# Projections of four attention stages: f32 products against three f16 products of split operands

## The chip, the core and the metric

One Trainium2 chip, one of its cores, one launch. The metric is the device time of that launch in microseconds (us).

## The reference, cut to what matters

Two decoder layers on `x` (8 blocks of 112 tokens, 256 wide) and a context (8 blocks of 375 tokens, 192 wide). Layer 0: feature-map attention, cross attention with a small feed-forward part, eight experts of which two serve each token. Layer 1 begins with squared-score attention, then wide cross attention, then causal attention with four small experts:

```python
# squared-score attention, 16 heads, 16 wide keys, 64 wide values
q, k, v = x @ Wq.T, x @ Wk.T, x @ Wv.T                 # 256, 256, 1024 wide
A = tril(1 + q.k / 4 + (q.k / 4) ** 2 / 2)
y = rms_norm(A @ v, per head) * g_weight
x = layernorm(x + y @ Wo.T)                            # 1024 -> 256
# wide heads: 16 heads, 64 wide, over the 375 context tokens
q = x @ w_q                                            # 256 -> 1024
x = layernorm(x + softmax(q.k / 8) @ v @ w_out + b)    # 1024 -> 256
# causal heads: 16 heads, 16 wide, rms norm in front and on queries and keys
h = rms(x) * n1_w
q, k, v = h @ wq.T, h @ wk.T, h @ wv.T                 # 256 each
```

The matrices named above, and the same `x` in front of them, are what the change is about.

## The kernel before, in words

A planner (`step`, `place`, `weave`, `rest`, `until`) writes one ordered list of units for each stage, `plans[0]` to `plans[5]`. Each engine (TensorE, ScalarE, VectorE, GpSimd, and SP, which issues most DMAs) walks the same list and issues its own part of every unit, so each engine's queue is strictly in the order of the list, and a wait holds everything behind it on that engine. Streams are woven by planned costs in ns (the last argument of `step`); `rest(ns)` lets so much planned cost pass before a stream goes on, and `REST` is 1500. Between two stages stands a fence: `end_stage` notes the last result of each of the four computing engines, and every engine waits for all of them (`fence`) before its first unit of the next stage.

**Stage 2** (`plans[2]`, to about 421 us of the profile) runs the eight experts. Its expert products are already three f16 products of split operands: a value times `WSCALE` is cast to f16, the rest of the cast is a second f16 tensor, and `PARTS` names the pairs high x high, high x low, low x high. Its last units are the last expert's output, and `get` 0 to 3, GpSimd's gathers of the experts' rows. The weights of the next stage are loaded by SP in `w3in`, and the context key weights are split in `wk4` (L1819, L1934).

**Stage 3** (`plans[3]`, 421 to 662 us) is the squared-score attention. First come the value units of the wide heads (`v4`, 5 products of 512 columns each, evicted by ScalarE at L624 and stored by DMA through four buffers), 18 of them ahead of the first `qk3`. Between them `combine` adds the gathered rows on VectorE (L2255), `norm` normalizes, and `xT`, `xTe` turn a block of `x` through TensorE into `x_ch`, channels on partitions, f32 (L587, ScalarE at L630). Then for each pair of blocks `qk3` (queries and keys, 224 columns), for each block `v3` (values, 512 columns), `s3` and `y3` (scores and sums), `turn3`, `sq3`, `rms3`, `scale3` (norm of the heads), `yT3`, `yT3e` (the turn of y into `s3_yT`, f32, ScalarE at L2242), and `out` (8 f32 products of 256 columns), followed by `norm` and the turn of the new `x`. The units `k4` (context keys of the wide heads, 5 f16 products of 375 columns) fill in between, and `wo3` lets GpSimd scale the output weight by `g_weight` once (L2313). All of `qk3`, `v3`, `out` and `q4` are f32 products; `mm` (L398) records all of them. Bank ring `misc3` has four banks.

**Stage 4** (`plans[4]`, 662 to 1024 us) weaves the wide heads with the causal ones. For each pair of heads: `sc4` (scores, L2604), the maximum on VectorE (L2684), the exponential on ScalarE (L2653), `nm4` (normalization on VectorE, L2695), `trA4`, `trV4` (turns, L2612, evicted by ScalarE at L2645 and by VectorE at L2676), `av4` (L2623); for each four pairs `oT4` (ScalarE evicts half a block's output into `s4_attT`, L2661); for each block `out`, `norm`, `xT`. `q4` makes the queries of two blocks. After a block's `norm` the causal heads follow: `qkv5` (three f32 projections of 256 columns), `ms5` (the mean squares on VectorE, and their power on GpSimd, L2985), `qk5`, `qkT5`, `s5`, `pT5`, `av5` and the rest. `n15` lets GpSimd scale the three weights of `qkv5` (L2714). `ffnin` loads the last stage's weights in three groups after the last `av4`.

**The order around the wide output.** `s4_out` waits in the plan for the second `oT4` of its block, then `rest(REST / 2)`, then places `out`. In the steady part of the list the units run `ms5` of an earlier block, `av4`, `oT4`, `sc4`, `pT5`, `av4`, `out`.

```python
def s4_out(b):
    yield from until(("oT4", b, 1))
    yield from rest(REST / 2)
    yield [("out", 4, b)]
    yield from norm_and_turn(4, b, pace=0.5)
```

## Time and profile before

| | |
|---|---|
| runs | 1168.29, 1170.60, 1169.72 us; median 1169.72 |
| profiled execution | span 1165.0 us (first to last instruction); its whole time is not listed apart from the three runs |
| instructions | 21556, of them 8624 matmul records |
| stage 3 | 421 to 662 us |
| stage 4 | 662 to 1024 us |

The times of the profile are microseconds from the first instruction. TensorE stands in two lines, PE for matmuls and PEld for weight loads, which overlap. DVE is VectorE, ACT is ScalarE, POOL is GpSimd. An f32 matmul of the program leaves two records, an f16 one leaves one. In brackets behind a row stands the idle time of the engine ahead of it and what ended it. The line number is the one of the helper that issues the instruction, so the tiles have to be read too: `w_Wo,s_yT` is the output of the squared-score heads, `w_Wv,x_ch` their values, `w_Wo,s_attT` the output of the wide heads, `x_ch,w_Wq` a query projection.

### The profile page before, as it was taken

How to read it: one execution, taken by the hardware profiler on the slowest of the kernel's cores; microseconds unless marked ns; L12 is line 12 of the kernel's file. 1: busy time of each engine (PE TensorE's matmuls, PEld its weight loads, DVE VectorE, ACT ScalarE, POOL GpSimd, SP SyncE). 2: the span in 40 equal slices, each digit the busy share in tenths (PEclk: the TensorE clock that was granted, in tenths of full speed). 3: DMA queues.
4: the chain of work that ended last, by engine and by line, in shares of the span. 5: the costliest groups of instructions: out<-in, count | busy, mean ns of one | idle time of the engine just before them, and what ended most of it. 6: DMA issues, size and time to landing. Idle time of an engine off the chain costs nothing.

```text
span 1165.0 us, 21556 instructions
## 1 busy us (share of the span) xinstructions
PE 1001.8 (86%) x8624; PEld 707.4 (61%) x8624; DVE 640.4 (55%) x1519; ACT 588.3 (50%) x1374; POOL 284.6 (24%) x292
## 2 busy tenths in 40 slices
PE   7996898887689988789998799889888897789995
PEld 4664565665388854456655676667666665447654
DVE  3246545666669833454455476776676664527003
ACT  5532565552468844344544354556555544465741
POOL 2521412100500033211112202221132124132733
PEclk9988889898989999899999988999999888679998
DMA  9341464102679785422252243313222105000001
GB/s 311 99 86 40 112 127 110 45 12 98 209 272 314 259 278 168 139 88 85 80 173 88 81 120 105 101 34 107 81 57 78 27 1 226 1 1 1 1 1 32
DMA packets 66676, 123.68 MB, mean 106 GB/s; under 512 B 11632, under 2 KB 41968, under 8 KB 62496
## 3 DMA queue, kind: packets, MB, share of 16 engines
q1 hardware_dynamic: 64528, 117.48, 33.0%
q0 software_dynamic: 2048, 4.82, 1.4%
q8 instruction: 68, 1.11, 0.4%
q14 instruction: 32, 0.26, 0.1%
HBM read 86.30 MB, written 35.92 MB: 105 GB/s over the span
## 4 chain that ended last, share of the span: by engine, by line
PE 56%; DVE 19%; ACT 11%; DMA 5%; issue 4%; POOL 4%; SPq 1%; another core or an unknown queue 0%; DVEq 0%; ACTq 0%; POOLq 0%
PE psum L398 38%; DVE s_p L2695 3%; ACT s_p L2653 3%; POOL rs L2985 2%; PE psum L2612 2%; DVE s_max L2684 2%; PE psum L2623 2%; PE psum L1369 2%; PE psum L2784 1%; DVE s_pT L2676 1%; PE psum L550 1%; DVE s_max L653 1%; PE psum L2173 1%; PE psum L2159 1%; PE psum L2604 1%
## 5 line engine op out<-in xcount | busy, mean ns | idle before, releaser
L2653 ACT ACTIVATE s_p<-psum,s_max 112x375 f32<-112x375 f32 x128 | 72.3, 569 | 87.6 <-DVE s_max L2684 87.6
L693 POOL TENSOR_TENSOR rstd<-meanvar,minus_half 112x1 f32<-112x1 f32 x40 | 23.1, 578 | 279.6 <-DVE meanvar L645 209.9
L653 DVE TENSOR_REDUCE s_max<-psum 112x2 f32<-112x750 f32 x64 | 59.4, 935 | 32.5 <-PE psum L550 31.4
L2985 POOL TENSOR_TENSOR rs<-ms,minus_half 112x32 f32<-112x32 f32 x8 | 43.5, 5442 | 110.3 <-DVE ms L2919 110.3
L398 PE MATMUL psum<-Wv,ctx 128*125 128x512 f16 x240 | 59.6, 392 | 11.2 <-ACT s_v L624 5.4
L398 PE MATMUL psum<-ctx,Wk 128*128 128x375 f16 x320 | 62.8, 331 | 5.0 <-ACT s_yT L2242 2.8
L2684 DVE TENSOR_REDUCE s_max<-psum 112x1 f32<-112x375 f32 x128 | 63.7, 539 | 2.3 <-PE psum L2604 2.1
L2612 PE MATMUL psum<-ident,s_p 112*125 112x112 f32 x384 | 61.4, 294 | 3.9 <-DVE s_p L2695 2.3
L609 ACT ACTIVATE s_k<-psum 128x375 f16<-128x375 f32 x64 | 31.2, 488 | 62.1 <-PE psum L398 59.5
L2604 PE MATMUL psum<-s_k,s_q 64*112 64x375 f16 x384 | 46.0, 345 | 17.0 <-ACT s_p L2653 6.5
L2612 PEld LDWEIGHTS psum<-ident,s_p 112*125 112x125 f32 x384 | 51.7, 198 | 13.7 <-DVE s_p L2695 3.9
L3303 POOL TENSOR_TENSOR hidden<-raw,hidden 128x448 f16<-128x448 f32 x44 | 45.6, 1036 | 54.4 <-ACT hidden L3186 52.7
L1431 ACT ACTIVATE s_pT<-psum 125x672 f32<-125x672 f32 x64 | 46.6, 730 | 22.8 <-PE psum L1357 21.2
L2623 PE MATMUL psum<-s_pT,s_v 125*64 125x112 f32 x768 | 53.9, 278 | 4.4 <-ACT s_attT L2661 4.4
L677 DVE SCALAR_TENSOR_TENSOR s_k<-psum,s_k 128x375 f16<-128x375 f32 x64 | 34.8, 546 | 36.2 <-ACT s_k L609 35.8
L624 ACT ACTIVATE s_v<-psum 125x512 f32<-125x512 f32 x48 | 28.3, 596 | 49.2 <-PE psum L398 33.4
L2623 PEld LDWEIGHTS psum<-s_pT,s_v 125*64 125x64 f32 x768 | 39.7, 143 | 20.1 <-issue 17.3
L398 PEld LDWEIGHTS psum<-Wv,ctx 128*125 128x125 f16 x240 | 32.1, 141 | 32.3 <-issue 9.6
L2695 DVE TENSOR_SCALAR s_p<-s_p,s_sum 112x375 f32<-112x375 f32 x128 | 49.3, 427 | 2.3
L3275 DVE SCALAR_TENSOR_TENSOR x_tok<-psum,wt,x_tok 112x192 f32<-112x192 f32 x32 | 12.6, 414 | 68.7 <-PE psum L398 68.6
L2645 ACT ACTIVATE s_pT<-psum 125x336 f32<-125x336 f32 x64 | 29.0, 453 | 38.3 <-PE psum L2612 38.2
L398 PE MATMUL psum<-x_ch,w_Wq 128*128 128x224 f32 x192 | 46.3, 382 | 2.1 <-ACT x_ch L630 1.5
(360 smaller groups left out, 2445.1 us busy)
## 6 DMA issues: line engine op xcount, KB each, us to landing
keys<-s_k SPq DMA_DIRECT2D x64, 187.5 KB, 2.2
s_k<-keys SPq DMA_DIRECT2D x8, 1500.0 KB, 7.6
values<-s_v SPq DMA_DIRECT2D x48, 224.0 KB
s_v<-values SPq DMA_DIRECT2D x16, 672.0 KB
raw_wg<-in_wg SPq DMA_DIRECT2D x8, 1024.0 KB, 6.6
raw_wu<-in_wu SPq DMA_DIRECT2D x8, 1024.0 KB, 7.1
raw_wd<-in_wd SPq DMA_DIRECT2D x8, 1024.0 KB
s_kd<-k_halves SPq DMA_DIRECT2D x48, 93.8 KB, 3.8
```

The costliest lines, as they stand in the source:

```text
L398: ins = TE.matmul(bank, left, right, start=i == 0, stop=last)
L653: VE.tensor_reduce(s1_max[b % 2][:, 2 * p:2 * p + 2], rings["s1"][unit][0:N, :, 0:S], X, ALU.max, negate=True).then_inc(*V.up("max1", n))
L677: VE.scalar_tensor_tensor(t[:, 1, :], rings["misc3"][unit][:, 0:S], 1 / WSCALE, t[:, 0, :], ALU.mult, ALU.subtract).then_inc(*V.up("k4", *at))
L1431: SC.activation(rings["pT1"][n], rings["s1"][unit][0:SCH, :, 0:NCH * N], ACT.Exp, scale=0.25).then_inc(*A.up("exp1", n))
L2604: ins = TE.matmul(rings["s4"][(n, j)][0:N, 0:S], q[rows, p, u, cols(b % 2)], k[rows, p, v, :], start=i == 0, stop=i == 2)
L2612: ins = TE.transpose(rings["t4"][unit][0:SCH, c * N:(c + 1) * N], p[:, c * SCH:(c + 1) * SCH], ident[0:N, 0:N])
L2623: ins = TE.matmul(rings["o4"][n // 4][64 * j:64 * j + 64, p % 4 * N:(p % 4 + 1) * N], s4_v[n // 4 % 3][:, c, 2 * (p % 4) + j, :], rings["p ...
L2653: SC.activation(rings["p4"][2 * n + j], rings["s4"][(n, j)][0:N, 0:S], ACT.Exp, bias=s4_max[b % 2][:, h:h + 1], accum_out=s4_sum[b % 2][:, ...
L2684: VE.tensor_reduce(s4_max[b % 2][:, h:h + 1], rings["s4"][(n, j)][0:N, 0:S], X, ALU.max, negate=True).then_inc(*V.up(name, n))
L2695: VE.tensor_scalar(t, t, sums[:, j:j + 1], None, ALU.mult).then_inc(*V.up(name, n))
L2985: GP.tensor_tensor(rs5[b % 2][:], ms5[b % 2][:], minus_half[:], ALU.pow).then_inc(*G.up("rs5", b))
L3303: GP.tensor_tensor(dst[:, 1, f, :], raw_, dst[:, 0, f, :], ALU.subtract).then_inc(*G.up("ll", *at))
```

## The change

All projections named in the reference above become three f16 products each. `x_ch` gives way, from the turn after the experts on, to `x16` in the same bytes: ScalarE casts the turned block to f16, VectorE writes the rest (`xH`, `xHe`); `s3_yT` is split in the same way (`yT3e` on both engines). The four weights of stage 3 are split by ScalarE and VectorE at the end of stage 2 (`w3s`, with `g_weight` in the scale of `Wo3`, so that `wo3` goes), those of the wide heads in stage 3 (`w4s`, after `out` of blocks 2 and 3), the three of the causal heads by GpSimd in `n15`, one block earlier than before. The output of the wide heads stays f32 in `s4_attT` and is split by GpSimd, a cast and a subtraction for each half (`oT4`); `out` waits for GpSimd and is placed `1.5 * REST` after `oT4`. Scales by 1/WSCALE go into the evictions. The third group of the last weights waits for the last wide `out`.

```diff
+    halves = Region(nc, keep.base + keep.at, KC * T_ * 4)
     x_ch = keep.tensor("x_ch", [P, KC, T_])
+    x16 = halves.tensor("x16", [P, 2, KC, T_], F16)
...
+    W3_16 = Region(nc, ringm.base + 28 * KB, 20 * KB)
+    w3_16 = {name: W3_16.tensor(name + "_16", shape, F16) for name, shape in (
+        ("Wv3", [P, 2, KC, HW]), ("Wq3", [P, 2, KC, D]), ("Wk3", [P, 2, KC, D]),
+        ("Wo3", [P, 2, HW // P, D]))}
...
-        return A["xT", s, b] if s >= 0 else g_x.ready
+        return V["xH", s, b] if s >= 2 else A["xT", s, b] if s >= 0 else g_x.ready
...
+    step("xH", "T xH", "misc#", "V xH", cost=250)
+    step("xHe", "A xH, V xH")
...
-            pe.wait_ge(x_ch_at(3, b), x_ch_at(3, b + 1), g_w4.ready, *ring.free(unit))
-            mm(ring[unit][:, 0:2 * N], [(Wq4[:, k, t * P:(t + 1) * P], x_ch[:, k, b * N:(b + 2) * N])
-                                        for k in range(KC)], T.up("q4", s, b, t))
+            pe.wait_ge(x_ch_at(3, b), x_ch_at(3, b + 1), V["w4s", "Wq4"], *ring.free(unit))
+            mm(ring[unit][:, 0:2 * N],
+               [(w4_16["Wq4"][:, u, k, t * P:(t + 1) * P], x16[:, v, k, b * N:(b + 2) * N])
+                for k in range(KC) for u, v in PARTS], T.up("q4", s, b, t))
...
+        if what == "xHe":
+            s, b = at
+            bank = rings[f"misc{s}"][("xH", s, b)]
+            act.wait_ge(T["xH", s, b])
+            SC.activation(x16[:, 0, :, cols(b)],
+                          bank[:, 0:KC * N].rearrange("p (t n) -> p t n", n=N),
+                          ACT.Copy).then_inc(*A.up("xH", s, b))
...
+    def vector_add_scaled(s, b, base, base_at, y):
+
+        dve.wait_ge(T["out", s, b], base_at)
+        VE.scalar_tensor_tensor(res[:, b, :], y, 1 / WSCALE, base[:, b, :], ALU.mult,
+                                ALU.add).then_inc(*V.up("nadd", s, b))
         dve.wait_ge(V["nadd", s, b])
         vector_moments(s, b, res)
...
+        if what == "xHe":
+            s, b = at
+            dve.wait_ge(A["xH", s, b])
+            VE.scalar_tensor_tensor(
+                x16[:, 1, :, cols(b)],
+                rings[f"misc{s}"][("xH", s, b)][:, 0:KC * N].rearrange("p (t n) -> p t n", n=N), 1.0,
+                x16[:, 0, :, cols(b)], ALU.mult, ALU.subtract).then_inc(*V.up("xH", s, b))
...
+    place(("g3",))
+    for name in ("Wq3", "Wk3", "Wv3", "Wo3"):
+        place(("w3s", name))
...
+            elif what == "w3s":
+                name, = at
+                act.wait_ge(g_w3.ready, T["down", E0 - 1], V["g3",])
+                SC.activation(w3_16[name][:, 0], w3[name][:], ACT.Copy,
+                              scale=ch("g3") if name == "Wo3" else WSCALE).then_inc(*A.up("w3s", name))
...
+            elif what == "w3s":
+                name, = at
+                dve.wait_ge(A["w3s", name], V["g3",])
+                VE.scalar_tensor_tensor(w3_16[name][:, 1], w3[name][:],
+                                        ch("g3") if name == "Wo3" else WSCALE, w3_16[name][:, 0],
+                                        ALU.mult, ALU.subtract).then_inc(*V.up("w3s", name))
...
+    raw_w4 = Region(nc, wts.base + keys_at, 20 * KB)
+    w4_raw = {"Wq4": g_w4.load(raw_w4, "Wq4", [P, KC, HW]),
+              "Wo4": g_w4.load(raw_w4, "Wo4", [P, HW // P, D])}
+    w4_16 = {"Wq4": ringm.tensor("Wq4_16", [P, 2, KC, HW], F16),
+             "Wo4": ringm.tensor("Wo4_16", [P, 2, HW // P, D], F16)}
...
-        place(("wo3",))
...
+        yield from until(("out", 3, 2))
+        yield [("w4s", "Wq4")]
+        yield from until(("out", 3, 3))
+        yield [("w4s", "Wo4")]
...
-                pe.wait_ge(g_w3.ready, x_ch_at(2, b), x_ch_at(2, b + 1), *rings["misc3"].free(unit))
-                for w, at_ in ((Wq3, 0), (Wk3, 2 * N)):
+                pe.wait_ge(x_ch_at(2, b), x_ch_at(2, b + 1), *rings["misc3"].free(unit))
+                for name, at_ in (("Wq3", 0), ("Wk3", 2 * N)):
                     mm(bank[:, at_:at_ + 2 * N],
-                       [(w[:, k, c * P:(c + 1) * P], x_ch[:, k, b * N:(b + 2) * N])
-                        for k in range(KC)], T.up("qk3", b, c) if at_ else None)
+                       [(w3_16[name][:, u, k, c * P:(c + 1) * P], x16[:, v, k, b * N:(b + 2) * N])
...
-                   [(x_ch[:, k, cols(b)], Wv3[:, k, c * 512:(c + 1) * 512]) for k in range(KC)],
-                   T.up("v3", b, c))
+                   [(x16[:, u, k, cols(b)], w3_16["Wv3"][:, v, k, c * 512:(c + 1) * 512])
+                    for k in range(KC) for u, v in PARTS], T.up("v3", b, c))
...
-                pe.wait_ge(A["yT3", b, 4], G["wo3",], *rings["misc3"].free(unit))
+                pe.wait_ge(V["yT3", b, 4], *rings["misc3"].free(unit))
                 mm(rings["misc3"][unit][0:N, 0:D],
-                   [(s3_yT[b % 2][:, k, :], Wo3[:, k, :]) for k in range(HW // P)], T.up("out", 3, b))
+                   [(s3_yT[b % 2][:, u, k, :], w3_16["Wo3"][:, v, k, :])
+                    for k in range(HW // P) for u, v in PARTS], T.up("out", 3, b))
             else:
...
+            elif what == "yT3e":
+                b, t0 = at
+                bank = rings["misc3"][("yT3", b, t0)]
+                dve.wait_ge(A["yT3", b, t0])
+                VE.scalar_tensor_tensor(s3_yT[b % 2][:, 1, t0:t0 + 4, :],
+                                        bank[:, 0:4 * N].rearrange("p (t n) -> p t n", n=N), 1.0,
+                                        s3_yT[b % 2][:, 0, t0:t0 + 4, :], ALU.mult,
+                                        ALU.subtract).then_inc(*V.up("yT3", b, t0))
...
+            elif what == "w4s":
+                name, = at
+                act.wait_ge(g_w4.ready, V["got", 2, B - 1])
+                SC.activation(w4_16[name][:, 0], w4_raw[name][:], ACT.Copy,
+                              scale=WSCALE).then_inc(*A.up("w4s", name))
...
+            elif what == "w4s":
+                name, = at
+                dve.wait_ge(A["w4s", name])
+                VE.scalar_tensor_tensor(w4_16[name][:, 1], w4_raw[name][:], WSCALE, w4_16[name][:, 0],
+                                        ALU.mult, ALU.subtract).then_inc(*V.up("w4s", name))
...
-            elif what == "wo3":
-                pool.wait_ge(g_w3.ready)
-                GP.tensor_scalar(Wo3[:], Wo3[:], ch("g3"), None, ALU.mult).then_inc(*G.up("wo3"))
...
+                sp.wait_ge(V["got", 2, B - 1])
...
-    step("oT4", "A oT4")
+    step("oT4", "A oT4, G +1, G oT4")
     step("w5in")
-    step("n15", "G +5, G n15")
+    step("n15", "G +9, G +2, G n15")
 
...
+        if b == 1:
+            place(("w5in",))
         if b == 2:
-            place(("w5in",))
+            place(("n15",))
         if b == 3:
-            place(("n15",))
             place(("ones5",))
...
-        yield from rest(REST / 2)
+        yield from rest(1.5 * REST)
...
-                pe.wait_ge(A["oT4", b, 1], *rings["misc4"].free(unit))
+                pe.wait_ge(G["oT4", b, 1], V["w4s", "Wo4"], *rings["misc4"].free(unit))
                 mm(rings["misc4"][unit][0:N, 0:D],
-                   [(s4_attT[:, k, :], Wo4[:, k, :]) for k in range(HW // P)], T.up("out", 4, b))
+                   [(s4_att16[:, u, k, :], w4_16["Wo4"][:, v, k, :])
+                    for k in range(HW // P) for u, v in PARTS], T.up("out", 4, b))
             elif what in UNITS5:
...
-                    act.wait_ge(T["out", 4, b - 1])
+                    act.wait_ge(G["oT4", b - 1, q])
...
+            elif what == "oT4":
+                b, q = at
+                half = slice(4 * q, 4 * q + 4)
+                if b:
+                    pool.wait_ge(T["out", 4, b - 1])
+                pool.wait_ge(A["oT4", b, q])
+                GP.tensor_copy(s4_att16[:, 0, half, :], s4_attT[:, half, :]).then_inc(*G.up())
+                pool.wait_ge(G.so_far())
+                GP.tensor_tensor(s4_att16[:, 1, half, :], s4_attT[:, half, :], s4_att16[:, 0, half, :],
+                                 ALU.subtract).then_inc(*G.up("oT4", b, q))
...
-                        w = ffn_w[name][:, c, :]
-                        GP.tensor_scalar(w, w, ch("n1", c), None, ALU.mult).then_inc(
-                            *(G.up("n15") if (name, c) == ("wv5", KC - 1) else G.up()))
+                        w = w5[name][:, c, :]
+                        GP.tensor_scalar(w, w, ch("n1", c), WSCALE, ALU.mult,
+                                         ALU.mult).then_inc(*G.up())
+                for name in ("wq5", "wk5", "wv5"):
+                    pool.wait_ge(G.so_far())
+                    GP.tensor_copy(w5_16[name][:, 0], w5[name][:]).then_inc(*G.up())
+                    pool.wait_ge(G.so_far())
+                    GP.tensor_tensor(w5_16[name][:, 1], w5[name][:], w5_16[name][:, 0],
+                                     ALU.subtract).then_inc(*(G.up("n15") if name == "wv5" else G.up()))
...
-                for group in ffn_groups:
+                for group in ffn_groups[:2]:
                     group.start()
+                sp.wait_ge(T["out", 4, B - 1])
+                ffn_groups[2].start()
...
-                   [(x_ch[:, k, cols(b)], ffn_w[w][:, k, :]) for k in range(KC)],
-                   T.up("qk5", b) if j else None)
+                   [(x16[:, u, k, cols(b)], w5_16[w][:, v, k, :])
+                    for k in range(KC) for u, v in PARTS], T.up("qk5", b) if j else None)
             pe.wait_ge(*ring.free(("vv5", b)))
             mm(ring[("vv5", b)][0:N, 0:D],
-               [(x_ch[:, k, cols(b)], ffn_w["wv5"][:, k, :]) for k in range(KC)], T.up("v5", b))
+               [(x16[:, u, k, cols(b)], w5_16["wv5"][:, v, k, :])
+                for k in range(KC) for u, v in PARTS], T.up("v5", b))
```

## Rows read from the trace of the kernel before

**Rows 1.** The page, part 1: busy time, its share of the span, instructions.

```profile
PE 1001.8 (86%) x8624; PEld 707.4 (61%) x8624; DVE 640.4 (55%) x1519; ACT 588.3 (50%) x1374; POOL 284.6 (24%) x292
```

**Rows 2.** The page, part 4: the chain that ended last, by engine.

```profile
PE 56%; DVE 19%; ACT 11%; DMA 5%; issue 4%; POOL 4%; SPq 1%; another core or an unknown queue 0%; DVEq 0%; ACTq 0%; POOLq 0%
```

**Rows 3.** Windows: stretch, length, busy us (instructions) by engine, PEclk, DMA share, GB/s.

```profile
490.00:640.00 150.00, 139.05 (x915) 87.79 (x916) 75.58 (x153) 68.87 (x149) 23.61 (x13) 1.00 0.32 103
640.00:662.00 22.00, 16.15 (x88) 13.49 (x88) 8.65 (x23) 6.73 (x18) 4.26 (x4) 1.00 0.03 10
...
760.00:960.00 200.00, 177.09 (x1560) 131.66 (x1556) 138.15 (x369) 111.34 (x362) 45.40 (x35) 0.96 0.19 55
960.00:1024.00 64.00, 45.65 (x296) 32.23 (x294) 28.05 (x60) 28.32 (x88) 19.88 (x17) 0.72 0.26 103
```

**Rows 4.** Timeline, TensorE, squared-score stage: start, us, line, what, records.

```profile
562.11 3.71 PE L398 MATMUL psum<-w_Wo,s_yT 128*112 128x256 f32 x16
...
572.39 1.02 PE L398 MATMUL psum<-x_ch,w_Wq 128*128 128x224 f32 x4
...
574.01 0.96 PE L398 MATMUL psum<-ctx,Wk 128*128 128x375 f16 x5
...
576.72 1.88 PE L398 MATMUL psum<-w_Wv,x_ch 128*112 128x512 f32 x4
```

**Rows 5.** Timeline, TensorE, queries of the wide heads, at the stage end.

```profile
645.25 3.95 PE L398 MATMUL psum<-x_ch,w_Wq 128*128 128x224 f32 x20
```

**Rows 6.** Timeline, TensorE, wide-head stage.

```profile
803.23 1.03 PE L398 MATMUL psum<-w_wk,x_ch 128*112 128x256 f32 x4
...
813.68 3.71 PE L398 MATMUL psum<-w_Wo,s_attT 128*112 128x256 f32 x16
```

**Rows 7.** Timeline, TensorE, f16 products of 256 columns.

```profile
137.37 0.71 PE L398 MATMUL psum<-Wkv,ctx 128*125 128x256 f16 x5
```

**Rows 8.** Timeline, TensorE, around the stage boundary.

```profile
421.32 8.82 PE L398 MATMUL psum<-Wv,ctx 128*125 128x512 f16 x40 [0.79 <-PE psum L1761]
...
449.92 0.99 PE L398 MATMUL psum<-x_ch,w_Wq 128*128 128x224 f32 x4 [1.46 <-ACT x_ch L630]
...
454.10 1.24 PE L398 MATMUL psum<-Wv,ctx 128*125 128x512 f16 x5
```

**Rows 9.** Timeline, ScalarE, around the stage boundary.

```profile
414.80 1.99 ACT L1819 ACTIVATE Wk<-Wk 128x1024 f16<-128x1024 f32 x2
...
420.63 0.59 ACT L1812 ACTIVATE e_out<-psum 70x512 f32<-70x512 f32 x1 [0.78 <-PE psum L1761]
```

**Rows 10.** Timeline, VectorE, around the stage boundary.

```profile
416.82 1.23 DVE L1934 SCALAR_TENSOR_TENSOR Wk<-Wk,Wk 128x1024 f16<-128x1024 f32 x1 [2.19 <-ACT Wk L1819]
...
430.94 0.48 DVE L2255 SCALAR_TENSOR_TENSOR res<-got,w_k,x_tok 112x256 f32<-112x256 f32 x1 [11.11 <-issue]
...
471.54 3.23 DVE L2277 SCALAR_TENSOR_TENSOR s_a<-s_a,half_causal 112x448 f32<-112x448 f32 x2 [1.68 <-ACT s_a L2221]
```

**Rows 11.** Timeline, GpSimd, around the stage boundary.

```profile
424.04 1.02 POOL L1965 DMA_INDIRECT got<-expert_out,get_i  x1 [52.23 <-DMA expert_out<-e_out]
...
470.03 5.45 POOL L2313 TENSOR_SCALAR w_Wo<-w_Wo,chan 128x2048 f32<-128x2048 f32 x1
```

**Rows 12.** One line (L2277): ns min/median/max of its instructions.

```profile
L2277 DVE SCALAR_TENSOR_TENSOR s_a<-s_a,half_causal x32: 611/622/2693, 462.7 to 626.2; 112x448 f32<-112x448 f32 x32
```

**Rows 13.** One line (L683): ns min/median/max.

```profile
L683 DVE SCALAR_TENSOR_TENSOR s_q<-psum,s_q x32: 379/391/393, 647.0 to 800.6; 128x224 f16<-128x224 f32 x32
```

**Rows 14.** Groups of GpSimd, by form: line, op, xcount, busy us, mean ns, idle.

```profile
L3303 POOL TENSOR_TENSOR hidden<-raw,hidden 128x448 f16<-128x448 f32 x44 | 45.6, 1036 | 54.4 <-ACT hidden L3186 52.7
...
L710 POOL CAST ctx<-ctx_raw 128x375 f16<-128x375 f32 x8 | 4.0, 499 | 27.9 <-DMA ctx_raw<-in_ctxT 19.8 <-PE psum L1357 8.1
```

**Rows 15.** Timeline, GpSimd, wide-head stage.

```profile
811.20 5.44 POOL L2985 TENSOR_TENSOR rs<-ms,minus_half 112x32 f32<-112x32 f32 x1 [17.54 <-DVE ms L2919]
```

**Rows 16.** Timeline, ScalarE, wide-head stage.

```profile
812.22 0.58 ACT L2661 ACTIVATE s_attT<-psum 128x448 f32<-128x448 f32 x1
```

69 lines of the change are left out of this document (42 added, 27 removed).

## The prediction, made before the changed kernel was run

> **What bounds the kernel now.** I read the busy shares first: TensorE 86%, every other engine far below [rows 1]. Then the chain that ended last: TensorE 56%, VectorE 19%, ScalarE 11% [rows 2]. TensorE is the first suspect, but almost half of the chain is somebody else's latency. So I cut the two stages that the change touches into windows [rows 3]. The squared-score stage is dense from 490 to 640 us (139.05 of 150 us busy, full clock) and loose at its end, 640 to 662 (16.15 of 22), where the last block goes through its chain alone. The wide-head stage has 177.09 of 200 us of TensorE, but VectorE has 138.15 beside it, and its 23 us of idle lie scattered between heads. Its tail, 960 to 1024, has TensorE busy 45.65 of 64 us at a mean clock of 0.72: latency again.
>
> A difference of 0.2% (2.3 us) is about what a measurement of this kernel can tell from none. The profiled span is 1165.0 us; its whole time is not listed. The three runs have a median of 1169.72, 4.7 above that span, and I sum against 1169.7.
>
> **What the products save.** A run in the timeline overlaps its successor by 0.16 us (its last end is modelled), so a run costs its length less 0.16. Each f32 matmul leaves two records.
> - Old output projection, 8 matmuls of 256 columns: 3.71 - 0.16 = 3.55 us; old values, 2 of 512 columns: 1.88 - 0.16 = 1.72; old query and key pair: 574.01 - 572.39 = 1.62 [rows 4]. Old wide queries: (3.95 - 0.16) / 5 = 0.76 each [rows 5]. One of the three last projections: 1.03 - 0.16 = 0.87; the wide output is again 3.55 [rows 6].
> - New price: an f16 product of 256 columns steps at (0.71 - 0.16) / 5 = 0.110 us [rows 7], one of 512 at (1.24 - 0.16) / 5 = 0.216 [rows 8]. Between them lies 0.41 ns a column, so 224 columns are 0.110 - 0.013 = 0.097.
>
> Three products replace each matmul:
> - squared-score output: 24 x 0.110 = 2.64 for 3.55, saves 0.91, x8 = 7.3
> - its values: 6 x 0.216 = 1.30 for 1.72, 0.42 x16 = 6.7
> - its queries and keys: 12 x 0.097 = 1.16 for 1.62, 0.46 x8 = 3.7
> - wide queries: 0.58 for 0.76, 0.18 x32 = 5.8, of which 8 units (1.4) fall in the squared-score stage and 24 (4.3) behind it
> - wide output: 0.91 x8 = 7.3
> - queries, keys, values of the causal heads: 18 x 0.110 = 1.98 for 2.61, 0.63 x8 = 5.0
>
> That is 19.1 us in the squared-score stage and 16.6 in the wide-head stage, 35.7 in all. Three quarters is what the rows give. The Trainium skill (FP8 and Floating Point Precision, TensorE Precision Notes) has f32 as four passes; three f16 passes are then exactly 25% less, and the rows agree within a few per cent.
>
> How much reaches the end? In the dense stretch TensorE idles 7%, so I take 0.9: 17 us (bounds 12 and 19). In the wide-head stage 11% idle sits between exponentials and maxima that the products don't shorten, so I take 0.75: 12.5 us (bounds 0, if the head loop is latency, and 19, with the halved clock of some stretches).
>
> **What it adds at the stage boundary.** The four weights of the squared-score stage are now split ahead of a fence that all engines wait for. ScalarE can begin after its last expert eviction, 421.2. It casts 5120 columns; two of 1024 took 1.99 us [rows 9], so 5.0 us, until 426.2. VectorE follows at 1.23 us per 1024 [rows 10]; its last 2048 begin after the last cast and end near 428.7. TensorE, which now starts 8 value units (40 products) at 421.32 [rows 8], idles 7.5 us. Is that the price? The layer's first combine waits for gathered rows until 430.94 [rows 10] on gathers that GpSimd issues from 424.04 [rows 11]; they are ahead of the fence and stay. But the first query unit, at 449.92, has 18 value units in front of it on TensorE. 428.7 + 18 x 1.08 = 448.1, plus 0.8 for turns and 1 for the split of x: 450, if the stores of the values keep up; in the kernel before the stretch of 18 units took 28.6 us instead of 20, and the clock may start low. Bounds 0 and +8; I take +4, the middle, since part of the old 28.6 us was the combine and part the stores.
>
> **Smaller terms.** GpSimd's scaling of the output weight goes, 5.45 us at 470.03 [rows 11]. During it a VectorE pair at 471.54 took 3.23 us [rows 10]; its instructions are 622 ns at the median and 2693 at most [rows 12]. That is 2 us on a stretch that TensorE waited for: -2 (bounds -3 and 0). The wide heads' two weights are split inside the stage: 2 casts of 1.9 us on ScalarE, 2 splits of 2.4 on VectorE, in queues ahead of key evictions; four banks cover about 3 us: +2 (0 to +5). Every turned block of x gets a VectorE split of 0.39 us [rows 13], 24 in all, every turned half of y one near 0.62 [rows 12], 16 in all; inside the dense stretch VectorE is half idle and they are covered, but in the last blocks' chains they are on the path: +2 (+1 to +5). The cast of x stays the same on ScalarE. SP's load of the wide weights now waits for the last combine, which is over by then: 0. The third group of the last weights waits for the last wide output; its queue is still busy with the first two: 0. The last projections' weights are split by GpSimd earlier, with one block more of lead: 0.
>
> **The wide heads' output, the new wait.** ScalarE evicts, then GpSimd casts (499 ns for 375 columns, so 0.6 for 448) and subtracts (1.036) [rows 14], and only then may TensorE run the output. The queue of GpSimd matters: its power of 5.44 us starts at 811.20 [rows 15], ScalarE evicts the block's second half at 812.22 [rows 16]; in five more blocks (from 737, 769, 851, 889 and 930 us) the same two stand within 1.2 us. So the split begins at 816.7 and ends at 818.4. The output stood at 813.68 [rows 6]. The order now places it behind 1500 planned ns more, about one transposed group, one attention step and one score, 2.6 us of TensorE: 816.3. TensorE then stands still 2.1 us, 6 times, 12.6 us, and scores, attention and turns of later heads are queued behind it. Some of that fills gaps that would come anyway: I take +9 (0 to +33). The 32 new GpSimd instructions also stand beside VectorE's: +2 (0 to +26). The tail after the last head: split of the attention +1.7, split of x +0.4, shorter products -1.5, later start of the last block's output: +1.
>
> **Sum.** 1169.7 - 17 - 12.5 + 4 - 2 + 2 + 2 + 9 + 2 + 1 = 1158.2; I say 1158.
>
> **The rivals.**
> - *The whole gain arrives.* The order moves the output far enough to hide the split, and gaps close: 1169.7 - 35.7 - 2 + 4 = 1136. For it: GpSimd is busy 24% and TensorE 86% [rows 1]. Against: gaps of latency. 20%.
> - *The head loop is latency.* The wide-head stage gives nothing back: 1158 + 12.5 = 1170.5. For it: TensorE has only 56% of the chain [rows 2]. 13%.
> - *Slower: the power in front of the split.* If the output keeps its real place, TensorE waits from 813.7 to 818.4, 4.7 us in 7 blocks, 33 us in place of 9: 1182. It decides from about 3.5 us of wait a block. For it: six blocks show the pair; against: three times the rest is planned ahead of the output. 12%.
> - *VectorE held up while GpSimd works.* One instruction was held 2 us beside a long one of GpSimd [rows 12]. Each block half would hold VectorE 1.64 us, 26 in all; half of it on the path is 13 in place of 2: 1169. Against: the normalization of the scores reads one tensor. The Trainium skill (SBUF — State Buffer, SBUF: two separate sides) speaks against this change: the port pair that VectorE and GpSimd share is an exclusive lock held for a whole instruction, taken by VectorE in a two-port mode or with two SBUF inputs. By that rule the 3.23 us are a lock (the trace agrees: 2693 ns for 622), and the new work would block alike. 11%.
> - *The forecast.* 44%.
>
> That the products aren't what they say can be left out: the lists are written out.
>
> **How the numbers follow.** Faster takes the forecast, the whole gain and a third each of the two rivals near 1170: 72%. Same 9%. Slower: the power, and the rest of those two, 19%. The range reaches from just above the whole gain to just above the latency case: 1140 to 1173.
>
> **What would show it.** Runs of 24 f16 records of 2.8 us for each output; the squared-score stage, from its first query unit to its end, shorter by 15 to 19 us; a first query unit between 450 and 458; TensorE idle ahead of the wide output, released by GpSimd, near 2 us in six blocks; VectorE's longest instructions beside GpSimd's copies no longer than 1 us. The forecast is wrong if that wait is absent or near 5 us, if the two stages shrink by much less than their products, or if the first query unit comes after 460.

## The result, and the profile after

The changed kernel takes 1201.61 us (median of 4 runs, 1198.83 to 1203.88) beside 1169.46 (4 runs), a ratio of 1.0252, 95% interval 1.0212 to 1.0292: **2.5% slower**, where 1158 was forecast and nothing above 1173 was in the range.

The page, part 1, of the changed kernel:

```profile
PE 992.4 (83%) x8928; PEld 711.2 (59%) x8928; DVE 671.4 (56%) x1566; ACT 592.9 (49%) x1380; POOL 309.4 (26%) x329
```

Beside [rows 1], TensorE is busy 9.4 us less and the span is 36.6 us longer. To find the place I cut both executions at the same events: the last eviction of expert outputs; the first query unit of the squared-score stage (its eviction, by VectorE); the first score of a wide head; the last transpose ahead of the last stage. Windows of the kernel before, squared-score and wide stretch (columns as in [rows 3]; the first number behind the bracket of GpSimd is PEclk, the clock that TensorE was granted, as a share of full speed):

```profile
451.70:661.70 210.00, 186.66 (x1151) 118.90 (x1150) 103.62 (x216) 88.47 (x193) 35.62 (x21) 0.98 0.30 97
661.70:1022.20 360.50, 309.97 (x2544) 229.70 (x2544) 234.21 (x613) 189.12 (x601) 83.13 (x73) 0.90 0.26 82
```

The changed kernel, boundary, squared-score and wide stretch:

```profile
425.10:463.30 38.20, 24.70 (x111) 14.70 (x112) 15.06 (x30) 16.56 (x25) 19.48 (x20) 0.87 0.65 199
463.30:688.30 225.00, 183.11 (x1292) 123.25 (x1290) 118.09 (x248) 91.54 (x195) 32.12 (x20) 0.91 0.27 90
688.30:1058.80 370.50, 301.52 (x2703) 228.16 (x2704) 244.13 (x621) 186.49 (x601) 110.01 (x111) 0.87 0.26 80
```

The boundary took 31.1 us before, the rest after the wide stretch 142.8 in both. So +7.1 at the boundary, +15.0 in the squared-score stretch, +10.0 in the wide one: 32.1, and the medians differ by 32.15. (The code ahead of the first cut is the same and took 420.6 and 425.1 us; over all executions below 415.6 to 426.2, so I take that part for scatter and compare stretches.)

Each stretch splits into TensorE's work at full clock (busy x granted clock, which its two digits give to about 1 us in the first stretch and 1.7 in the second), what the lower clock adds, and idle:

| | work | busy | clock | idle |
|---|---|---|---|---|
| squared-score, before | 182.9 | 186.7 | 0.98 | 23.3 |
| squared-score, after | 166.6 | 183.1 | 0.91 | 41.9 |
| wide, before | 279.0 | 310.0 | 0.90 | 50.5 |
| wide, after | 262.3 | 301.5 | 0.87 | 69.0 |

The products saved what they should: 16.3 us of work in the first stretch and 16.7 in the second, where 19.1 and 16.6 were forecast. But idle rose by 18.6 and 18.5, and the lower granted clock took most of what the products had saved: 166.6/0.91 is 13 us more than 166.6/0.98, and 262.3/0.87 is 10 us more than 262.3/0.90. TensorE's waits, longest first, in the squared-score stretch of the kernel before (line, releaser, us, times, longest):

```profile
PE psum L398 <- ACT s_yT L2242: 6.4, 8, 1.5
PE psum L587 <- DVE x_tok L688: 2.5, 1, 2.5
...
PE psum L2189 <- ACT s_yT L2242: 2.2, 2, 1.6
PE psum L398 <- ACT x_ch L630: 2.1, 3, 1.0
...
PE psum L2159 <- ACT s_yT L2242: 2.0, 2, 1.0
```

and in that of the changed kernel:

```profile
PE psum L405 <- DVE s_yT L2371: 13.1, 8, 2.6
PE psum L405 <- DVE x L714: 5.9, 3, 3.5
PE psum L2216 <- DVE s_yT L2371: 5.2, 4, 1.9
PE psum L598 <- DVE x_tok L721: 4.3, 2, 2.5
PE psum L2246 <- DVE s_yT L2371: 3.8, 2, 2.2
```

L2371 is VectorE's subtraction of the turned y. Scores (L2216) and turns (L2246) don't read y at all: they wait for its **PSUM bank**, the slot of the ring `misc3` in which TensorE had left the turned y. So do most of the waits at L405, the line of all products: in the timeline six of its eight stand ahead of context keys and values (10.0 us), and only two ahead of an output (3.1 us, 1.6 before). In all, the waits that end with y's eviction grew from 10.6 us in 12 to 22.1 in 14. The bank was waited for before the change too. One such place in both kernels, TensorE (start, us, what, [idle before <- releaser]), before:

```profile
539.69 1.01 PE L2159 MATMUL psum<-s_q,s_k 32*112 32x224 f32 x8 [1.01 <-ACT s_yT L2242]
```

after:

```profile
550.81 1.01 PE L2216 MATMUL psum<-s_q,s_k 32*112 32x224 f32 x8 [0.71 <-DVE s_yT L2371]
...
556.29 1.61 PE L2216 MATMUL psum<-s_q,s_k 32*112 32x224 f32 x8 [1.89 <-DVE s_yT L2371]
```

and VectorE:

```profile
554.26 0.69 DVE L2347 TENSOR_REDUCE s_ms<-s_y 112x8 f32<-112x512 f32 x1
554.95 0.55 DVE L703 SCALAR_TENSOR_TENSOR s_k<-psum,s_k 128x375 f16<-128x375 f32 x1
555.53 0.17 DVE L2352 TENSOR_SCALAR s_ms<-s_ms 112x16 f32<-112x16 f32 x1
555.62 0.62 DVE L2371 SCALAR_TENSOR_TENSOR s_yT<-psum,s_yT 128x448 f16<-128x448 f32 x1
```

ScalarE's eviction from that bank ran 554.81 to 555.35. In the kernel before it freed the bank; now the bank stays until 556.24, and TensorE stands 1.89 us, of which about 1.0 would have been there with ScalarE's mark. The 0.89 us that are new are 0.62 of the subtraction itself and 0.27 in VectorE's queue. In the first 14 of the 16 halves the subtraction began 0.02 to 0.45 us behind ScalarE's end, 3.0 us in all, and took 8.6 us itself: it is mostly the length of the new reader that holds the bank, and not the queue in front of it.

The second new wait is for `x`: products wait 5.9 us for VectorE's half of it (L714), where they waited 2.1 for the eviction, and turns of `x` wait 4.3 us for VectorE's norm (L721), 2.5 before.

The boundary, TensorE:

```profile
424.40 0.63 PE L1799 MATMUL psum<-ident,e_dT 128*70 128x128 f32 x4 [1.04 <-ACT e_dT L1842]
433.29 8.54 PE L405 MATMUL psum<-Wv,ctx 128*125 128x512 f16 x30 [8.26 <-DVE Wo L1980]
...
461.99 0.73 PE L405 MATMUL psum<-x,Wq 128*128 128x224 f16 x6 [1.60 <-DVE x L714]
```

8.26 us idle (7.5 forecast), and the first 30 records come at 8.54 us, where 40 took 8.82 in [rows 8]. Windows right behind the idle time show why (changed kernel):

```profile
433.30:438.00 4.70, 4.70 (x14) 2.64 (x15) 2.77 (x8) 0.99 (x2) 3.48 (x5) 0.60 0.32 99
438.00:442.00 4.00, 3.82 (x18) 2.14 (x16) 2.73 (x9) 1.99 (x4) 3.41 (x4) 1.00 0.87 231
```

The granted clock is 0.60 in the first, most of it at the 1.2 GHz level, and 1.00 in the second.

The wide stage. TensorE:

```profile
854.35 2.83 PE L405 MATMUL psum<-Wo,s_att 128*112 128x256 f16 x24
...
1007.36 4.36 PE L405 MATMUL psum<-Wo,s_att 128*112 128x256 f16 x24 [2.72 <-POOL s_att L2799]
```

GpSimd:

```profile
845.65 5.44 POOL L3088 TENSOR_TENSOR rs<-ms,minus_half 112x32 f32<-112x32 f32 x1 [17.83 <-DVE ms L3022]
...
851.55 0.56 POOL L2797 CAST s_att<-s_attT 128x448 f16<-128x448 f32 x1
852.19 1.04 POOL L2799 TENSOR_TENSOR s_att<-s_attT,s_att 128x448 f16<-128x448 f32 x1
```

The pair behind the power is there as forecast, yet in most blocks TensorE does not wait: the later place hides it (7.1 us in 3 waits, L405 <- L2799, in the whole stretch). So what cost the rest of the 18.5 us of idle, and the clock? The waits name a part of it: causal scores wait 6.5 us for exponentials (L2885 <- L2735; 1.7 before), the causal turns 5.2 us for ScalarE (L2894 <- L2974; 0.6 before), while a wait of 5.1 us of the wide scores for VectorE is gone. The rest is spread over many short ones. VectorE at the same time:

```profile
851.63 1.81 DVE L2777 TENSOR_SCALAR s_p<-s_p,s_sum 112x375 f32<-112x375 f32 x2
```

An undisturbed pair takes 0.74 us, this one took 1.81 beside GpSimd's two instructions; over the kernel their mean rose from 427 to 481 ns, 6.9 us for 128 (441 in e2 and 484 in e6 below, which differ by GpSimd's split). The Trainium skill (SBUF — State Buffer, SBUF: two separate sides) describes a port pair shared by VectorE and GpSimd as an exclusive lock that is held for a whole instruction. The stretched pair agrees with a lock; "for a whole instruction" does not hold for every instruction here: beside GpSimd's power of 5.44 us, in the kernel before, eight such pairs took their 0.74 us each.

### The profile page after: what moved, and what is told of

The parts are those of the page before. It is cut to its first block, busy times and chain, and to the rows that moved or that the text cites. A ratio compares the mean times of both kernels' runs of the same rounds, so it can differ in the third digit from the quotient of the medians.

```text
span 1201.6 us, 22274 instructions
## 1 busy us (share of the span) xinstructions
PE 992.4 (83%) x8928; PEld 711.2 (59%) x8928; DVE 671.4 (56%) x1566; ACT 592.9 (49%) x1380; POOL 309.4 (26%) x329
## 4 chain that ended last, share of the span: by engine, by line
PE 53%; DVE 19%; ACT 12%; DMA 6%; issue 4%; POOL 4%; SPq 1%; another core or an unknown queue 0%; DVEq 0%; ACTq 0%; POOLq 0%
PE psum L405 36%; ACT s_p L2735 3%; DVE s_p L2777 3%; PE psum L2704 2%; PE psum L2693 2%; DMA raw_wd<-in_wd 2%; POOL rs L3088 2%; DVE s_max L2766 2%; PE psum L2885 1%; PE psum L1402 1%; PE psum L2216 1%; DVE s_pT L2758 1%; PE psum L2230 1%; DMA values<-s_v 1%; PE psum L2685 1%
## 5 line engine op out<-in xcount | busy, mean ns | idle before, releaser
L2735 ACT ACTIVATE s_p<-psum,s_max 112x375 f32<-112x375 f32 x128 | 72.1, 568 | 100.1 <-DVE s_max L2766 100.1
L726 POOL TENSOR_TENSOR rstd<-meanvar,minus_half 112x1 f32<-112x1 f32 x40 | 24.8, 620 | 270.9 <-DVE meanvar L671 197.5
L405 PE MATMUL psum<-Wv,ctx 128*125 128x512 f16 x240 | 62.7, 409 | 17.2 <-DVE Wo L1980 8.3
L405 PE MATMUL psum<-ctx,Wk 128*128 128x375 f16 x320 | 66.5, 346 | 10.1 <-DVE s_yT L2371 6.6
L620 ACT ACTIVATE s_k<-psum 128x375 f16<-128x375 f32 x64 | 31.1, 487 | 66.9 <-PE psum L405 66.5
L2693 PEld LDWEIGHTS psum<-ident,s_p 112*125 112x125 f32 x384 | 53.5, 206 | 17.2 <-DVE s_p L2777 8.7
L2704 PE MATMUL psum<-s_pT,s_v 125*64 125x112 f32 x768 | 56.5, 287 | 5.9 <-ACT s_attT L2743 5.9
L2777 DVE TENSOR_SCALAR s_p<-s_p,s_sum 112x375 f32<-112x375 f32 x128 | 56.2, 481 | 2.3
L405 PEld LDWEIGHTS psum<-Wv,ctx 128*125 128x125 f16 x240 | 33.7, 147 | 39.0 <-issue 20.7
L703 DVE SCALAR_TENSOR_TENSOR s_k<-psum,s_k 128x375 f16<-128x375 f32 x64 | 34.7, 546 | 38.7 <-ACT s_k L620 38.2
L3378 DVE SCALAR_TENSOR_TENSOR x_tok<-psum,wt,x_tok 112x192 f32<-112x192 f32 x32 | 12.6, 414 | 68.7 <-PE psum L405 68.6
L405 PEld LDWEIGHTS psum<-ctx,Wk 128*128 128x128 f16 x320 | 30.1, 102 | 33.9 <-DVE s_yT L2371 8.1
L2727 ACT ACTIVATE s_pT<-psum 125x336 f32<-125x336 f32 x64 | 29.1, 455 | 37.2 <-PE psum L2693 37.1
```

The lines of the kernel that those rows point to most:

```text
L405: ins = TE.matmul(bank, left, right, start=i == 0, stop=last)
L703: VE.scalar_tensor_tensor(t[:, 1, :], rings["misc3"][unit][:, 0:S], 1 / WSCALE, t[:, 0, :], ALU.mult, ALU.subtract).then_inc(*V.up("k4", *at))
L2693: ins = TE.transpose(rings["t4"][unit][0:SCH, c * N:(c + 1) * N], p[:, c * SCH:(c + 1) * SCH], ident[0:N, 0:N])
L2704: ins = TE.matmul(rings["o4"][n // 4][64 * j:64 * j + 64, p % 4 * N:(p % 4 + 1) * N], s4_v[n // 4 % 3][:, c, 2 * (p % 4) + j, :], rings["p ...
L2735: SC.activation(rings["p4"][2 * n + j], rings["s4"][(n, j)][0:N, 0:S], ACT.Exp, bias=s4_max[b % 2][:, h:h + 1], accum_out=s4_sum[b % 2][:, ...
L2777: VE.tensor_scalar(t, t, sums[:, j:j + 1], None, ALU.mult).then_inc(*V.up(name, n))
```

## The experiments

Seventeen kernels ran, each with two timed executions or more (e2 and e11 with 8, e5 with 10, e16 with 11, e12 with 12). The stretches, each of one profiled execution, and the ratio of the times to the kernel before on the same chip:

| run | boundary | squared | wide | ratio (95%) |
|---|---|---|---|---|
| before | 31.1 | 210.0 | 360.5 | |
| after | 38.2 | 225.0 | 370.5 | 1.0252 (1.021-1.029) |
| e1_y_f32 | 34.4 | 210.2 | 369.6 | 1.0146 (1.004-1.025) |
| e2_wide_f32 | 36.7 | 224.8 | 345.2 | 1.0123 (1.007-1.018) |
| e3_four | 36.8 | 236.6 | 383.7 | 1.0514 (1.035-1.068) |
| e4_wo3_late | 34.5 | 228.6 | 370.5 | 1.0298 (1.019-1.041) |
| e5_both_f32 | 35.6 | 212.2 | 346.5 | 0.9982 (0.994-1.002) |
| e6_split_unused | 36.1 | 221.9 | 353.2 | 1.0148 (1.007-1.023) |
| e7_rest | 36.5 | 224.7 | 364.9 | 1.0249 (1.018-1.032) |
| e8_wide_sv | 37.3 | 222.7 | 362.1 | 1.0266 (1.020-1.033) |
| e9_split_early | 36.8 | 222.7 | 377.5 | 1.0377 (1.030-1.045) |
| e10_y_hold | 34.2 | 225.9 | 349.7 | 1.0101 (1.003-1.017) |
| e11_y_sbuf | 37.1 | 217.3 | 342.9 | 1.0061 (1.002-1.010) |
| e12_wide_queries | 31.0 | 216.6 | 347.8 | 0.9949 (0.992-0.998) |
| e13_late_even | 36.6 | 222.7 | 357.9 | 1.0224 (1.017-1.028) |
| e14_mid_even | 37.3 | 226.3 | 362.8 | 1.0246 (1.018-1.032) |
| e15_wide_f32_late_even | 37.4 | 220.9 | 360.4 | 1.0212 (1.015-1.027) |
| e16_queries_no_rest | 34.3 | 211.6 | 364.4 | 1.0081 (1.005-1.012) |
| e17_before_late | 37.2 | 210.9 | 370.8 | 1.0119 (1.004-1.020) |

How far is a stretch to be trusted? The same squared-score code (y split, Wo3 split ahead) took 220.9 to 226.3 us in nine executions, the same wide code 369.6 to 370.5 in three and 342.9 to 349.7 in four. The boundary of the kernel before took 31.1 and, in e17, 37.2; e12 and e16, with the same boundary, took 31.0 and 34.3. So a difference under 7 us between two stretches is not read by itself. The runs are of several chips, and a single profile can lie off its own times: that of e2 was 3.0 us longer than that of the kernel before, while its ratio says 14. So each main reading is given below by the ratios too; 1% is 11.7 us.

In the diffs, `...` stands for lines left out; they are against the changed kernel where nothing else is said.

**e1_y_f32**: y and the squared-score output product stay f32, the bank is released by ScalarE.

```diff
-    step("yT3", "T yT3", "misc3", "V yT3", 500)
-    step("yT3e", "A yT3, V yT3")
+    step("yT3", "T yT3", "misc3", "A yT3", 500)
+    step("yT3e", "A yT3")
...
-                   [(s3_yT[b % 2][:, u, k, :], w3_16["Wo3"][:, v, k, :])
-                    for k in range(HW // P) for u, v in PARTS], T.up("out", 3, b))
+                   [(s3_yT[b % 2][:, k, :], Wo3f[:, k, :])
+                    for k in range(HW // P)], T.up("out", 3, b))
```

> The squared-score output alone goes back to f32: y is turned and kept in f32, its bank is released by ScalarE, the output weight is one scaled f32 cast, and VectorE's 16 splits of y are gone; all else stays changed. Theory 1 (a turn's bank in the four-bank ring is now held until VectorE's split, TensorE stands still for it and its clock falls): the 22 us that TensorE waited for the split of y shrink to about 10 behind ScalarE's eviction, the mean granted clock from the first query unit to the stage's end rises from 0.91 to 0.96 or more, and the stage loses 10 to 18 us: about 1187. Theory 2 (fewer passes alone let the clock fall, waits are incidental): TensorE's work grows by 7 us, the waits don't matter, at most 4 us are gained: 1197 or more.

The stretch fell by 14.8 us, to 210.2, though its output products are longer again; by the ratios (1.0252 to 1.0146, with intervals that touch) it is 12. The granted clock is 0.96 for 0.91. The waits that end with y's eviction are back to 10.5 us, the longest group being (TensorE, squared-score stretch):

```profile
PE psum L406 <- ACT s_yT L2306: 6.3, 7, 1.5
```

That is the first theory. But 210.2 is also what the kernel before takes, with 11.8 us more of products in its stretch by the steps of the prediction: something besides y takes those.

**e2_wide_f32**: the wide output in f32 as before, without GpSimd's split, at its old place.

```diff
-    step("oT4", "A oT4, G +1, G oT4")
+    step("oT4", "A oT4")
...
-        yield from rest(1.5 * REST)
+        yield from rest(REST / 2)
...
-                   [(s4_att16[:, u, k, :], w4_16["Wo4"][:, v, k, :])
-                    for k in range(HW // P) for u, v in PARTS], T.up("out", 4, b))
+                   [(s4_attT[:, k, :], w4_16["Wo4"][:, k, :])
+                    for k in range(HW // P)], T.up("out", 4, b))
```

> The wide heads' output alone goes back to f32, without GpSimd's split and with the old rest ahead of it. Theory 1: the 7 us that TensorE waited for GpSimd's split go, and what the clock lost behind them; the wide-head stage (373 us, 363 before the change) comes back to 363 to 367: 1193 to 1197. Theory 2: the output is 0.9 us longer in each block and nothing else changes: 1205.

25.3 us less in the wide stretch, far more than either theory had; by the ratios, 1.0252 to 1.0123, it is 15. So this half of the change cost 15 to 25 us, although 7 us of saved product are in it.

**e3_four**: a fourth product (low by low) added to every split projection, work that the kernel does not need.

```diff
+FOUR = PARTS + ((1, 1),)
...
-                for k in range(KC) for u, v in PARTS]
+                for k in range(KC) for u, v in FOUR]
```

> Every changed projection gets the fourth product, low times low, so TensorE has the passes of f32 again (about 36 us more at full clock), with every wait of the change kept. Theory 1: the time is set by waits in part; the longer products are partly hidden and the clock is granted a little more often, so 10 to 25 us are added: 1212 to 1226. Theory 2: the clock comes back to 0.98 in the squared-score stage, which gives back what the products cost, so the time stays within 5 us of 1201.

By the steps of [rows 7, 8] it adds 35.6 us of TensorE, 18.6 and 17.0 in the two stretches; they grew by 11.6 and 13.2, 24.8 in all (30 by the ratios), as the first theory had it. TensorE's work does count, at 0.6 and 0.8 of its length. The gain was not lost because TensorE is off the path.

**e4_wo3_late**: the split of the squared-score output weight is moved behind the fence.

```diff
-    for name in ("Wq3", "Wk3", "Wv3", "Wo3"):
+    for name in ("Wq3", "Wk3", "Wv3"):
         place(("w3s", name))
...
         yield from until(("norm", 2, B - 1))
+        place(("wo3s",))
         place(("w4in",))
```

> The split of the squared-score output weight moves from ahead of the fence to where the kernel before scaled it (after the last norm of the layer before), so that the fence opens 1.9 us of ScalarE and 2.35 us of VectorE less late. Boundary theory: the first value unit and the first query unit come 2 to 4 us earlier, and the two instructions cost at most 1 us at their new place: 1197 to 1200. If the value units' stores or the combine set the first query unit, it stays at 36 us behind the start of the last expert eviction: 1201.

3.7 us less at the boundary and 3.6 more behind it, both under the scatter, and no difference in the time. The four kernels without VectorE's split of that weight ahead of the fence (e1, e4, e5, e10) have boundaries of 34.2 to 35.6, those with it 36.1 to 38.2: about 2 us.

**e5_both_f32**: e1 and e2 together.

> Both outputs (squared-score and wide) back to f32 with their old queues, all other projections stay f16 products. If the two costs are independent, the stages are those of the two single undoings: 210 us from the first query unit to the first score, 345 to the last stage; with 34 ahead and 143 behind them that is 12 us less than the same four stretches of the kernel before (744.4), so 1.0% faster than it, ratio 0.99. If the chip's clock or the ring simply shifts the idle time elsewhere, the sum stays above 740: ratio 1.0.

1162.87 us against 1163.95: no difference, over 10 and 13 runs, where the stretches of the two single undoings had promised 1%. So splitting the two outputs' operands, with the later place of the wide one, costs the whole 2.5%. But the other projections, 21.1 us of forecast product, bring nothing that the times can tell: their boundary is 4.5 us longer, their squared-score stretch 2.2 us longer, and only the wide one 14.0 shorter. Its windows, squared-score and wide:

```profile
461.10:673.30 212.20, 182.77 (x1229) 119.24 (x1228) 107.47 (x231) 91.28 (x195) 30.19 (x21) 0.94 0.29 95
673.30:1019.80 346.50, 290.90 (x2639) 217.39 (x2640) 237.65 (x621) 187.75 (x601) 84.95 (x79) 0.93 0.28 85
```

**e6_split_unused**: e2, and GpSimd splits the wide operand into a place that nobody reads. Against e2:

```diff
-    step("oT4", "A oT4")
+    step("oT4", "A oT4, G +1, G oT4")
...
-                    act.wait_ge(T["out", 4, b - 1])
+                    act.wait_ge(T["out", 4, b - 1], G["oT4", b - 1, q])
...
+                GP.tensor_copy(s4_att16[:, 0, half, :], s4_attT[:, half, :]).then_inc(*G.up())
+                pool.wait_ge(G.so_far())
+                GP.tensor_tensor(s4_att16[:, 1, half, :], s4_attT[:, half, :], s4_att16[:, 0, half, :],
+                                 ALU.subtract).then_inc(*G.up("oT4", b, q))
```

> The kernel with the wide output in f32, plus GpSimd's 32 instructions that split the attention, whose result nobody reads or waits for. Port theory (GpSimd's cast and subtraction hold VectorE's normalization, and push GpSimd's own powers back): the wide-head stage grows from 345 to 355 or more. Wait theory (what cost time was TensorE waiting for the split and its later place): it stays within 3 us of 345.

353.2 against 345.2, 8 us for 32 instructions that nobody waits for but ScalarE, a block later, and one late load; the same code without them took up to 349.7 (e10), and by the ratios, whose intervals overlap, it is 3 us. Between the two theories, and small.

**e7_rest**: e2, and only the place of the product moved. Against e2:

```diff
-        yield from rest(REST / 2)
+        yield from rest(1.5 * REST)
```

> The kernel with the wide output in f32, but the output placed 1.5 rests behind the eviction as in the change, not half a rest. If the later place costs (it moves each block's causal heads later in the list and lengthens the tail), the wide-head stage grows from 345 to 350 or more; if it only made room for the split, it stays within 2 us of 345.

This was the surprise. The same instructions on every engine, one number of the planner changed, and the stretch grew by 19.7 us (15 by the ratios, 1.0123 to 1.0249, whose intervals just stand apart). Window of e2:

```profile
679.70:1024.90 345.20, 290.40 (x2640) 217.55 (x2640) 237.53 (x621) 187.39 (x601) 85.20 (x79) 0.93 0.28 85
```

Window of e7:

```profile
680.20:1045.10 364.90, 303.29 (x2640) 226.94 (x2640) 238.38 (x621) 186.78 (x601) 84.49 (x79) 0.89 0.27 81
```

The work is 270 us in both (290.4 x 0.93, 303.3 x 0.89). 12.9 us come from the granted clock and 6.8 from idle. The causal scores' wait of 6.5 us and their turns' of 5.2 are here too (1.4 and 0.6 in e2), without any split of the operand: these belong to the place.

**e8_wide_sv**: the changed kernel, the wide operand split by ScalarE (high) and VectorE (low, from the bank) instead of GpSimd, at the old place.

```diff
-    step("oT4", "A oT4, G +1, G oT4")
+    step("oT4", "A oT4, V oT4")
...
-                    rings["o4"].take(o // 4, (A, ("oT4", o // HP, o % HP // 4)))
+                    rings["o4"].take(o // 4, (V, ("oT4", o // HP, o % HP // 4)))
...
-        yield from rest(1.5 * REST)
+        yield from rest(REST / 2)
...
-                SC.activation(s4_attT[:, 4 * q:4 * q + 4, :],
+                SC.activation(s4_att16[:, 0, 4 * q:4 * q + 4, :],
...
+                VE.scalar_tensor_tensor(s4_att16[:, 1, 4 * q:4 * q + 4, :],
+                                        rings["o4"][2 * b + q][:, 0:4 * N].rearrange("p (t n) -> p t n", n=N), 1.0,
+                                        s4_att16[:, 0, 4 * q:4 * q + 4, :], ALU.mult,
+                                        ALU.subtract).then_inc(*V.up("oT4", b, q))
```

> The changed kernel with the wide output's split done by ScalarE (cast) and VectorE (rest) straight from the bank, as for y, with the old rest; GpSimd has no part in it, and the bank of the attention is released by VectorE. Port and wait theories of GpSimd both say that the stage falls below 370; if VectorE, busy 66% of this stage, and the bank held longer cost as in the squared-score stage, it lands between 350 and 365, and not at 345, although the output's products are 7 us shorter.

362.1, within the 350 to 365 of the second expectation. The stretch is shorter than with GpSimd at either place, but the time is not (ratio 1.0266, the changed kernel's is 1.0252), and it is 17 us worse than no split, by the stretches and by the ratios alike. The attention step waits for VectorE 10.1 us in 14 times at the start of a bank that ScalarE freed before (3.3 us in 4 times in e2). The profile puts these waits down to L2773, the instruction right behind the subtraction in VectorE's queue; that they are the same kind of loss as in the squared-score stage is read from the edit, not shown by a run of its own.

**e9_split_early**: the changed kernel with its product at the old place.

```diff
-        yield from rest(1.5 * REST)
+        yield from rest(REST / 2)
```

> The changed kernel with one number put back: the wide output product rests REST/2 again instead of 1.5*REST, so the planner lays it out where the kernel before has it, while GpSimd still splits its operand. The wide heads' stretch (first wide score to the last transpose ahead of the last stage) took 370.5 us in the changed kernel and 360.5 before. Theory A (the later place is what costs: without GpSimd's split the same move took the stretch from 345.2 to 364.9 us): about 350 to 358 us here, since TensorE's output comes down to f16 as well. Theory B (the later place was needed to hide GpSimd's two instructions of 1.6 us per half): the wait of the output product on GpSimd grows from 7.1 us to some 15 to 25 us and the stretch stays at 370 us or goes above it.

It took 377.5: theory B, and not the 350 to 358 of theory A. TensorE, wide stretch:

```profile
PE psum L405 <- POOL s_att L2799: 24.3, 6, 5.1
```

That is the slower rival's wait, six blocks of 4 us. So the later place was needed for the split: the ratio is 1.0377 without it and 1.0252 with it. But it hides 17.2 us of waits (24.3 to 7.1) for a stretch that is only 7.0 us shorter.

**e10_y_hold**: e5, and VectorE reads the bank of y once more for a result that nobody uses; it releases the bank, the output waits for ScalarE alone. Against e5:

```diff
-    step("yT3", "T yT3", "misc3", "A yT3", 500)
-    step("yT3e", "A yT3")
+    step("yT3", "T yT3", "misc3", "V yT3", 500)
+    step("yT3e", "A yT3, V yT3")
...
+                VE.scalar_tensor_tensor(s3_lo[:, t0:t0 + 4, :],
+                                        bank[:, 0:4 * N].rearrange("p (t n) -> p t n", n=N), 1.0,
+                                        s3_yT[b % 2][:, t0:t0 + 4, :], ALU.mult,
+                                        ALU.subtract).then_inc(*V.up("yT3", b, t0))
```

> The version with both f32 outputs (squared-score stretch 212.2 us), plus VectorE's subtraction of the squared-score operand from its PSUM bank, written to a place that nobody reads; the bank is released by VectorE, the output product waits for ScalarE alone. Theory A (the loss of 15 us in that stretch comes from the bank being held until VectorE is done and from VectorE's queue): 220 to 226 us. Theory B (it comes from the output product waiting for VectorE's half): 212 to 215 us.

225.9 against 212.2, and by the ratios 14 us: the whole loss, with an output product whose operand waits for nothing new. TensorE's waits that end with the new reader:

```profile
PE psum L406 <- DVE s_lo L2380: 9.7, 6, 2.6
...
PE psum L2223 <- DVE s_lo L2380: 5.2, 4, 1.9
PE psum L2253 <- DVE s_lo L2380: 3.8, 2, 2.2
```

With 1.7 us for ScalarE's half they are 20.4 us, where e5 has 10.6. These 9.8 us are the growth of idle (29.4 to 39.2); the other 4.0 of the 13.7 are the granted clock, 0.94 to 0.92. So it is the bank, and the clock behind it.

**e11_y_sbuf**: e2 (y split, output in f16), but ScalarE evicts twice, f32 and f16, and frees the bank; VectorE subtracts from the f32 copy. Against e2:

```diff
-    step("yT3", "T yT3", "misc3", "V yT3", 500)
-    step("yT3e", "A yT3, V yT3")
+    step("yT3", "T yT3", "misc3", "A yT3", 500)
+    step("yT3e", "A +1, A yT3, V yT3")
...
+                SC.activation(s3_yf[:, t0:t0 + 4, :],
+                              bank[:, 0:4 * N].rearrange("p (t n) -> p t n", n=N),
+                              ACT.Copy).then_inc(*A.up())
...
-                                        bank[:, 0:4 * N].rearrange("p (t n) -> p t n", n=N), 1.0,
+                                        s3_yf[:, t0:t0 + 4, :], 1.0,
```

> The squared-score operand is split again and its output product is in f16 (the wide output in f32, squared-score stretch 224.8 us), but the PSUM bank is released by ScalarE: it evicts the operand twice, in f32 to SBUF and in f16, and VectorE subtracts from the f32 copy. The output product still waits for VectorE. Theory A (bank held): the stretch falls to 208 to 214 us, a little of it lost to 16 more evictions of about 0.6 us on ScalarE. Theory B (output waits for VectorE's queue): it stays at 222 to 228 us.

217.3: VectorE has the same work, the output still waits for it, and 7.5 of the 12.6 us between e2 and e5 come back with the bank; the ratio falls from 1.0123 to 1.0061 (7 us; the intervals overlap). It lies between the two theories: ScalarE's second eviction holds the bank in its turn, so that 13.9 us of waits still end with ScalarE, and the outputs wait 4.7 us for VectorE.

**e13, e14, e15.** The planner's lists, and the timelines of the kernels before and after with them, showed what 1.5 x REST does besides: the scores of causal batches 0 to 4 stand at wide heads 25, 33, 41, 47, 57 instead of 25, 32, 40, 48, 56. With 1.25 and 2.5 x REST the step is even again. e13 is the changed kernel at 2.5, e14 at 1.25, e15 is e2 at 2.5.

```diff
-        yield from rest(1.5 * REST)
+        yield from rest(2.5 * REST)
```

> The changed kernel with 2.5*REST instead of 1.5*REST ahead of the wide output product. By the planner's order the score products of the causal batches 0 to 4 then stand at wide heads 26, 33, 41, 49, 57 (an even step of 8, as with REST/2: 25, 32, 40, 48, 56), where 1.5*REST puts them at 25, 33, 41, 47, 57 (steps of 6 and 10). Theory C (the uneven rhythm of the causal heads among the wide ones is what the later place costs; GpSimd's split is hidden at 1.5*REST and beyond): the wide stretch falls from 370.5 to 350 to 358 us. Theory L (every step that the output product, and so the tail of the causal stage, comes later costs): 370 us or more.

> The changed kernel with 1.25*REST: the causal batches' scores stand at wide heads 25, 32, 40, 48, 56, just as with REST/2, and the output product up to one head later than with REST/2. Theory C: the wait on GpSimd is between the 24.3 us of REST/2 and the 7.1 us of 1.5*REST, with the even rhythm kept: stretch 355 to 366 us, below both neighbours (377.5 and 370.5). Theory L: between its neighbours, 371 to 377 us.

> The version with the wide output in f32 and without GpSimd's split (stretch 345.2 us at REST/2, 364.9 at 1.5*REST), at 2.5*REST: late, with the even rhythm. Theory C: 345 to 351 us. Theory L: 365 us or more.

Rests of 0.5, 1.25, 1.5 and 2.5 REST give 377.5, 362.8, 370.5 and 357.9 us with the split, and 345.2, (not run), 364.9 and 360.4 without. With the split, the uneven place is the worst of the later three, by 8 to 13 us; without it, it is only 4.5 us worse than 2.5, which itself costs 15. The two stretches with the split lie where theory C had them, e15 lies between C and L. By the ratios none of the steps of the rhythm can be told from nothing: 1.0246 and 1.0224 beside 1.0252 with the split, 1.0212 beside 1.0249 without. So that the rhythm is a part is not shown; being elsewhere than at REST/2 is the larger part, and the one that the ratios show (e7).

**e12_wide_queries**: only the part that splits no output's operand and no weight ahead of the fence: wide queries and causal projections in f16; the squared-score stage in f32, both halves of x in the bytes of their own batch so that f32 and f16 blocks of x can live side by side.

```diff
-    x16 = halves.tensor("x16", [P, 2, KC, T_], F16)
+    x16 = halves.tensor("x16", [P, KC, B, 2, N], F16)
...
-    unit, ended = ("xT", "xTe") if s < 2 else ("xH", "xHe")
+    unit, ended = ("xT", "xTe") if s < 3 else ("xH", "xHe")
...
-    for name in ("Wq3", "Wk3", "Wv3", "Wo3"):
-        place(("w3s", name))
```

> Only the part of the change that costs no wait: the wide queries and the causal projections as three f16 products, everything of the squared-score stage in f32 as before (no weight split ahead of the fence), the wide output in f32 at its old place. By the stretches: boundary 31 us as before (the version with both f32 outputs has 35.6), squared-score 210 (212.2), wide 345 to 347 (360.5 before). So 1146 to 1152 us, ratio 0.985 to 0.990. If the wide stretch's gain were an accident of the order of work rather than 9 us less TensorE work and a higher granted clock, it would go back to 355 to 360 and the ratio to 0.995 to 1.000.

1161.30 us (12 runs) against 1164.68 (23 runs), a ratio of 0.9949 with an interval of 0.992 to 0.998: a little **faster than both kernels**, by 0.5% at this ratio and by 0.3% at the plain medians, where 1.0 to 1.5% were expected. Its wide stretch (347.8 against 360.5) alone would give 1.1%; its squared-score stretch took 216.6 in this execution and 211.6 in e16, with the same code.

**e16_queries_no_rest, e17_before_late**: e12 with no rest at all (the diff), and the kernel before with 1.5 x REST.

```diff
-        yield from rest(REST / 2)
+        yield from rest(0.0)
```

> The version with the wide queries alone in f16 (ratio 0.9949, wide stretch 347.8 us at REST/2) with no rest at all ahead of the wide output product; the product comes one head earlier for batches 0 to 2. Theory L (each step that it comes later costs): an earlier place keeps or gains, 340 to 347 us, ratio 0.988 to 0.994. Otherwise (REST/2 is the best place, since there the operand has just been evicted): waits on ScalarE's eviction of the operand ahead of the product, 350 to 356 us, ratio 1.000 or more.

> The kernel before with one number changed, 1.5*REST ahead of the wide output product. If the place is a cost of its own whatever the operands, its wide stretch goes from 360.5 to 375 to 381 us and the ratio to 1.012 to 1.018. If it was harmful only beside the shorter f16 queries, the stretch stays within 355 to 365 and the ratio within 0.995 to 1.005.

Both lose: 364.4 against 347.8, and 370.8 against 360.5; by the ratios 15 us (0.9949 to 1.0081) and 14 (1.0119). In e17 the window reads:

```profile
674.00:1044.80 370.80, 317.16 (x2544) 235.18 (x2544) 234.62 (x613) 187.82 (x601) 82.70 (x73) 0.87 0.26 79
```

So "later costs" falls too: an earlier place costs as much. The place is a cost of its own in the kernel before, and without the split REST/2 is the best of those tried. Of e17's 10.3 us, 7.2 are the granted clock and 3.1 idle; the causal scores' wait of 6.5 us and their turns' of 5.2 are there again. Why each other place draws a lower granted clock (0.87 in e17, 0.88 in e16, 0.89 in e7, 0.90 in e15; 0.90, 0.92 and 0.93 at REST/2 in the kernel before, e12 and e2) I can't say: each is below the same code at REST/2, and no single wait in them carries it. That stays open.

## Why the prediction was wrong, by its steps

- **What the products save** held. An output run of 24 f16 records takes 2.83 us (2.64 + 0.16 forecast). Work at full clock fell by 16.3 and 16.7 us for 19.1 and 16.6. The shares that reach the end, 0.9 and 0.75, stand beside 0.6 and 0.8, at which e3's added work arrives, so the first was high. In e5's wide stretch, where no output is split, 14 us arrived (360.5 to 346.5) for 9.3 of forecast products, since the granted clock rose there from 0.90 to 0.93.
- **The boundary**: +4 (0 to +8) forecast, +7.1 measured. The first query unit came at 461.99, past the 460 that I had called the mark, but 4.5 us of that lie ahead of the boundary, where the code is the same; from the last expert eviction it came 7.6 us later than before. Idle time was right (8.26 for 7.5); the slow clock behind it was named but not priced. The kernel before's own boundary took 31.1 and, in e17, 37.2 us (at a granted 0.77), so the term is 1 to 7.
- **The step that failed first** is the sentence on the turned halves of y: "inside the dense stretch VectorE is half idle and they are covered", +2 for all splits. I priced the subtraction by how busy VectorE is and never asked who waits for what it releases. It frees a bank of a ring of four for which TensorE already waited in the kernel before, 10.6 us in 12 times; so nearly every one of the 16 subtractions came on top: 22.1 us of waits now, and 4 us or more of clock. Measured: +12.6 to +14.8 us by the stretches of e1, e5 and e10, 12 to 16 by the ratios.
- **The step that failed second** is the place of the wide output. The prediction took the 1500 planned ns as pure shelter, "the order now places it behind 1500 planned ns more", and gave the move no price. It costs 10.3 us in the kernel before (e17) and 19.7 in e2's stage (e7), 14 to 15 in both by the ratios. The wait itself was over-priced: 7.1 us in 3 waits, where 2.1 us in each of six blocks were forecast and 9 us taken.
- **A term that the sum did not have** is the granted clock behind the boundary. The squared-score stage was read as "dense from 490 to 640 us (139.05 of 150 us busy, full clock)" and that clock taken over for the changed kernel without a term for it. The clock went from 0.98 to 0.91 in the squared-score stretch and from 0.90 to 0.87 in the wide one, 13 and 10 us of the 32. Undoing y's split gives the first back in part (0.96 in e1), undoing the wide half the second (0.93 in e2). Why the clock falls with the order is open.
- **The split of x** shared the +2 with that of y. Products wait 5.9 us for VectorE's half of x where they waited 2.1 for the eviction, +3.8 in the squared-score stretch; turns of x wait 4.3 us for VectorE's norm, 2.5 before. No run took it alone.
- **GpSimd beside VectorE**: +2 (0 to +26) forecast, 3 to 8 in e6. "No longer than 1 us" for VectorE's longest instruction beside GpSimd's copies was wrong: one normalization took 1.20 us between 840 and 860 us, 1.31 at most in the stage, and a pair 1.81. So was the reading of the lock in the rival: the pair that took 3.23 us ended at 474.77, while GpSimd's instruction of 5.45 us ran on to 475.48, and pairs beside the power took their usual time.
- **GpSimd's scaling that goes, the weights of the wide heads**: no run took them alone.
- **The rivals.** "The power in front of the split" (12%) is what e9 shows at the old place, 24.3 us in 6 waits, with a ratio of 1.0377; the changed kernel escapes it and pays by the move. Two terms that none of the rivals held, the bank and the place with the clock of both, took the gain. Sum by the two profiles: squared-score, -16.6 for the work (at the old clock), +13 clock, +18.6 idle (11.5 of it y's release, 5.6 the waits around x); wide, -18.5 for the work, +10 clock, +18.5 idle (7.1 of it GpSimd's split); boundary +7.1. By the ratios: y's half 12 to 16 us, the wide half 15, everything else together nothing (e5). And 0.2%, the prediction's mark for a difference that a measurement can tell, was too hopeful: the medians of the kernel before were 1159.38 to 1175.07 us in the later sessions.

## What to carry to other kernels

When a change moves the last reader of a PSUM bank (or of any ring slot) to another engine, look in the old trace whether the next user of the slot already waits for it. If it does, the new reader's whole length, and whatever stands in front of it in its engine's queue, goes on the path, however idle that engine is: here 16 subtractions of 0.62 us, the first 14 begun at most 0.45 us behind ScalarE, cost 12 to 16 us with the clock. Free the bank with the first eviction if that engine has room, but a second eviction holds it too: in e11 about half of the loss came back. An operation moved in an order that was tuned to the others is not free either: move it alone first, in the old kernel, and measure. And take a change of many parts apart before giving it up: the part that splits no output made the kernel 0.3 to 0.5% faster.

## What the runs showed of the hardware

- The granted clock is a term of the sum here. With the same instructions in another order, e2 and e7 differ by 0.93 and 0.89 in the wide stretch, 12.9 us of 19.7. In 20 us pieces the clock of e7 falls to 0.74 to 0.85 between 200 and 280 us into the stretch, where e2 has 1.00. In the squared-score stretch it was 0.96 to 0.98 with f32 projections (four executions) and 0.90 to 0.96 with f16 ones.
- After 8.26 us without work TensorE's next 4.7 us ran at a granted clock of 0.60 and held 14 f16 records of 512 columns (0.34 us each), against 0.22 at full clock: some 1.9 us lost beside the idle time.
- A GpSimd cast and subtraction (0.56 and 1.04 us) stretched a VectorE pair from 0.74 to 1.81 us. GpSimd's power of 5.44 us left eight such pairs at 0.74 us in the kernel before.
